# Layer 1 of a two-layer graph network: the sixth gather of a block becomes a table product, ScalarE makes half of the selection matrices, and the bias products change places

## What is computed

```python
h = jnp.maximum(_layernorm(x, axis=-1), 0.0)
x = x + segment_sum(h[src] * edge_weight[:, None], dst)            # layer 0
h = jnp.maximum(_layernorm(x, axis=-1), 0.0)
# layer 1, for each edge e with source row h[src] = (s: 8 scalars, v: 8 vectors of 3)
hid = relu(edge_attr_32 @ W1 + b1)                                 # 32 -> 64
w = (hid @ W2 + b2).reshape(e, 4, 8, 8)                            # 64 -> 256: four 8x8 matrices
m0 = ALPHA * (einsum('ei,eio->eo', s * sh0, w_000) + C110 * einsum('eim,em,eio->eo', v, sh1, w_110))
m1 = ALPHA * (einsum('ei,em,eio->eom', s, sh1, w_011) + einsum('eim,eio->eom', v * sh0, w_101))
x = x + concat(segment_sum(m0, dst), segment_sum(m1, dst)) + self-interaction of h
```

## Time and profile before

| | us |
|---|---|
| median of 3 runs | 6377.49 |
| lowest, highest | 6376.77, 6378.89 |
| the profiled execution, its own time | 6384.63 |
| its span, first to last instruction | 6382.8 |

### The profile page before, as it was taken

One profiled execution on the slowest core, in us unless ns is written; L12 is line 12 of the kernel. 1 busy time (PEld: TensorE's weight loads), 2 busy tenths in 40 slices (PEclk: granted clock), 3 DMA queues, 4 the chain that ended last, 5 costly groups with the idle time before them and its releaser, 6 DMA issues.

```text
span 6382.8 us, 156934 instructions
## 1 busy us (share of the span) xinstructions
PE 6036.7 (95%) x42909; PEld 4954.4 (78%) x42909; DVE 5681.9 (89%) x13211; ACT 2874.3 (45%) x12179; POOL 4754.2 (74%) x5071
## 2 busy tenths in 40 slices
PE   5999999999999999996999999999999999999998
PEld 5888888888888888884777777777777777777775
DVE  7888887777778777776999999999999999999997
ACT  2222222222222222225556556556565565555655
POOL 4777777777777777776777777777777777777776
PEclk9999999999999999997999999999999999999998
DMA  4111111111111111112111111111111111111111
GB/s 109 34 34 34 34 34 34 32 33 34 34 34 34 32 33 34 34 30 45 38 38 38 40 39 38 39 38 38 39 38 38 40 39 39 39 38 38 39 38 34
DMA packets 293179, 243.21 MB, mean 38 GB/s; under 512 B 106611, under 2 KB 289619, under 8 KB 292679
## 3 DMA queue, kind: packets, MB, share of 16 engines
q0 software_dynamic: 158848, 81.65, 9.5%
q1 hardware_dynamic: 133500, 158.02, 9.3%
q10 hardware_dynamic: 802, 3.22, 0.2%
HBM read 237.26 MB, written 5.25 MB: 38 GB/s over the span
## 4 chain that ended last, share of the span: by engine, by line
DVE 26%; PE 25%; POOL 24%; issue 21%; DVEq 3%; DMA 1%; POOLq 1%; ACT 0%; SPq 0%; ACTq 0%
POOL z L464 24%; PE w_ps L705 11%; PE hp_ps L856 6%; DVE prod L1189 5%; DVE p L1174 4%; PE w_ps L786 3%; DVE t L1205 3%; DVE z L1240 3%; DVE prod L1181 3%; DVE reduced_sb L1151 2%; DVE vsh L1167 1%; DVE reduced_sb L1150 1%; DVE prod L1210 1%; DVEq L1002 1%; DVE acc L1009 1%
## 5 line engine op out<-in xcount | busy, mean ns | idle before, releaser
L464 POOL DMA_INDIRECT z<-h_table,idx x4964 | 4710.1, 949 | 1556.6 <-issue 1473.9
L705 PE MATMUL w_ps<-parts,pick 128*128 128x448 f32 x12180 | 2561.6, 369 | 69.5 <-DVE pick L1019 65.6
L705 PEld LDWEIGHTS w_ps<-parts,pick 128*128 128x128 f32 x12180 | 2268.5, 188 | 278.7 <-issue 75.3
L566 ACT ACTIVATE z<-z,squares 128x32 f32<-128x32 f32 x3132 | 726.8, 309 | 2064.6 <-DMA z<-h_table,idx 1951.8
L856 PE MATMUL hp_ps<-parts,pick 128*128 128x448 f32 x6020 | 1341.4, 373 | 32.2 <-DVE squares L1233 29.6
L856 PEld LDWEIGHTS hp_ps<-parts,pick 128*128 128x128 f32 x6020 | 1096.7, 188 | 269.2 <-DVE squares L1233 126.4
L786 PE MATMUL w_ps<-w_sb,squares 64*128 64x256 f32 x6264 | 1088.0, 386 | 0.7 <-ACT squares L617 0.7
L786 PEld LDWEIGHTS w_ps<-w_sb,squares 64*128 64x128 f32 x6264 | 921.9, 194 | 60.2 <-ACT squares L617 1.2
L1019 DVE TENSOR_TENSOR pick<-sc_ps,feat 128x896 fp32r<-128x896 f32 x870 | 911.4, 1081 | 3.6 <-PE w_ps L705 3.6
L1181 DVE TENSOR_TENSOR prod<-w_ps,squares 128x384 f32<-128x384 f32 (+1 forms) x1044 | 781.0, 748 | 0.7 <-ACT squares L623 0.7
L620 ACT ACTIVATE scalars<-z 128x48 f32<-128x48 f32 x522 | 150.9, 289 | 1307.9 <-DMA z<-h_table,idx 1307.8
(11 more groups left out here) (91 smaller groups left out, 4716.4 us busy)
## 6 DMA issues: line engine op xcount, KB each, us to landing
z<-h_table,idx POOLq DMA_INDIRECT x4964, 2.4
squares<-in_ft_sh SPq DMA_DIRECT2D x261, 216.0 KB
feat<-key_table SPq DMA_DIRECT2D x260, 192.0 KB
feat<-key_table SPq DMA_DIRECT2D x260, 128.0 KB
h_table<-big SPq DMA_DIRECT2D x10, 280.0 KB
rel_sb<-in_dst_t SPq DMA_DIRECT2D x1, 1566.0 KB, 10.8
idx_all<-in_src_t SPq DMA_DIRECT2D x1, 1530.0 KB, 9.0
squares<-in_ew_t SPq DMA_DIRECT2D x1, 1530.0 KB, 12.6
```

Source lines behind the costliest of these rows:

```text
L464: pool.indirect_dma_start(z[:, r, u, :], None, rows, bass.IndirectOffsetOnAxis(ap=idx[:, r, u:u + 1], axis=0)).then_inc(z_in[r], 16)
L566: last = nc.scalar.activation(z[:, r, u, :], z[:, r, u, :], ACT.Copy, scale=ew_all[:, bass.ds(n * G + u, 1)])
L705: mm = pe.matmul(fold_ps[:, pick_banks[k], 0:NC * D], pick[:, k, blk, :], parts[:, t, :, blk, :], start=(blk == 0 and t == 0), stop=(blk = ...
```

## The change

Five edits, all in layer 1.

1. Table product in every step: `on_pe` and PE1 are gone. POOL fetches five tiles in the sixth step of a block too; PE, `select` and `sum_groups1` work in all six.
2. Selection matrices by two engines: those of the steps 1, 3 and 5 of a block are made by ACT (`rows_away`: seven activations of 128x128, minus the distance of row number and key, then one of 128x896, relu of one minus that distance), those of steps 0, 2 and 4 by DVE as before. `pick` is used as a ring of three slots in place of five.
3. The comparison `group1_hot` moves from `select` to the head of DVE's step, behind `vsh`.
4. All three biases of a step run on `halves[q]`, in the order third bank, bank 1 - q, then the hidden product, then bank q. The wait for `wts_used` goes ahead of the hidden product, and PE waits for its own bias (`bias_put`) behind the first weight product.
5. SP loads the keys in two lots of three, after waits for two selection matrices each.

```diff
-PE1 = R1 - 1
+RING1 = 3
...
+    def pick_by_act(r):
+        return r % 2 == 1
+    def pick_turn(b, r):
+        return (b - 1) * (R1 // 2) + r // 2 + 1
...
     def arrivals(b, r):
-        return 16 * (G + b * (GT if on_pe(r) else G))
+        return 16 * (G + b * GT)
...
                     if s is None or s >= R1:
-                        sp.wait_ge(pick1_ready, nth(b, 0) + at + count)
-                        sp.nop(nofuse=True)
-                    load_keys1(n - r + R1, at, count)
+                        for t in (at + 1, at + 2):
+                            sp.wait_ge(pick1_by_act if pick_by_act(t) else pick1_by_dve, pick_turn(b, t))
+                            sp.nop(nofuse=True)
...
             def tiles1(r, s):
-                return GT if on_pe(r) and (s is None or s >= R1) else G
+                return GT if s is None or s >= R1 else G
...
+            def rows_away(b, t, s):
+                act.wait_ge(keys1_in[t // BATCH], b * 16)
+                if s is None or s + 4 >= R1 + RING1:
+                    act.wait_ge(picked1, nth(b, t) - RING1 + 1)
+                off = pick[:, t % RING1]
+                for blk in range(GB):
+                    last = nc.scalar.activation(off[:, blk, :], key1[:, t], ACT.Abs, scale=-1.0, bias=rows_sb[:, blk:blk + 1])
+                last.then_inc(rows_off, 1)
+                act.wait_ge(rows_off, pick_turn(b, t))
+                nc.scalar.activation(off, off.bitcast(F32), ACT.Relu, scale=-1.0, bias=one_sb[:]).then_inc(pick1_by_act, 1)
...
                     copy_indices(n + R1, r, idx1_ready)
+                bt, t = before(b, r, R1, -4)
+                if pick_by_act(t) and (s is None or R1 <= s + 4 < S):
+                    rows_away(bt, t, s)
...
                 tile_weights(q, 2, turn, halves[turn], 2, False).then_inc(half_ready, 1)
+                pe.wait_ge(bias_put, n + 1)
...
                     bias(q, 2, halves[q])
+                    if s is None or s >= 2:
+                        pe.wait_ge(wts_used, n - 1)
+                    bias(q, 1 - q, halves[q]).then_inc(bias_put, 1)
...
                         hidden((r + 1) % R1).then_inc(hidpre_ready, 1)
-                    if s is None or s >= 2:
-                        pe.wait_ge(wts_used, n - 1)
                     bias(q, q, halves[q])
-                    bias(q, 1 - q, halves[1 - q])
...
-                if on_pe(t) and (s is None or R1 <= s + 2 < S):
+                if s is None or R1 <= s + 2 < S:
...
-                            mm = pe.matmul(picked_ps, pick[:, t, blk, :], parts[:, p, :, blk, :],
+                            mm = pe.matmul(picked_ps, pick[:, t % RING1, blk, :], parts[:, p, :, blk, :],
...
                         ALU.mult).then_inc(prod_step, 1)
+                mark()
                 step(1)
...
-                nc.vector.tensor_tensor(group1_hot[:], iota_sb[:, 0:NC], group_of[:, bass.ds(b * R1 + r + 2, 1)].to_broadcast([P, NC]),
-                                        ALU.is_equal).then_inc(group1_step, 1)
                 dve.wait_ge(picked1, i + 1)
...
-                    if on_pe((r + 4) % R1) and (s is None or R1 <= s + 4 < S):
+                    if not pick_by_act((r + 4) % R1) and (s is None or R1 <= s + 4 < S):
                         make_pick1(b, r, s)
```

More of the change, by code:

```diff
@@ L250, in gnn_two_layers @@
         table1_in, split1_act, split1_dve = sem("table1_in"), sem("split1_act"), sem("split1_dve")
-        pick1_ready, picked1, group1_step, selected1 = (
-            sem(n) for n in ("pick1_ready", "picked1", "group1_step", "selected1"))
+        pick1_by_dve, pick1_by_act, rows_off, picked1, group1_step, selected1 = (
+            sem(n) for n in ("pick1_by_dve", "pick1_by_act", "rows_off", "picked1", "group1_step", "selected1"))
         idx1_ready, z1_in = (sems(n, R1) for n in ("idx1_ready", "z1_in"))
@@ L282, in groups @@
                         body(g * GU + k, k, False, g)
-        assert JG * D == P and G == 6 and 4 * WN == 1024 and 3 * BATCH > PE1 > BATCH
+        assert JG * D == P and G == 6 and 4 * WN == 1024 and R1 == 2 * BATCH == 2 * RING1 and SLOTS >= RING1
         def stage_columns(op, n, k, js, staged):
@@ L421, in load1 @@
                     sp.dma_start(ft_sh_sb[:, r // 2, :], ft_sh[pair]).then_inc(ft_in[r // 2], 16)
[L423 to L426, removed]
                 if r >= R1 - 2 and (s is None or s - r + R1 < S):
+                    at = 0 if r == R1 - 2 else BATCH
                     if s == R1 - 2:
@@ L640, in prepare @@
                         act.wait_ge(wts_used, m - 1)
-                    if on_pe(v) and (t is None or t >= R1):
+                    if t is None or t >= R1:
                         act.wait_ge(selected1, nth(bv, v) + 1)
@@ L782, in bias @@
             def bias(q, k, rows):
-                pe.matmul(weight_bank(q, k), ones_sb[rows, :], b2_rows[rows, :], start=True, stop=False)
+                return pe.matmul(weight_bank(q, k), ones_sb[rows, :], b2_rows[rows, :], start=True, stop=False)
             def tile_weights(q, k, place, rows, column, stop):
@@ L850, in edge_layer @@
                         pe.wait_ge(split1_dve, 2)
-                    pe.wait_ge(pick1_ready, i + 1)
+                    pe.wait_ge(pick1_by_act if pick_by_act(t) else pick1_by_dve, pick_turn(bt, t))
                     if s is None or s + 2 > R1:
@@ L878, in wide_weights @@
                 pe.nop(nofuse=True)
-                for k in range(3):
-                    bias(0, k, halves[k % 2])
+                bias(0, 0, halves[0])
+                bias(0, 2, halves[0])
+                bias(0, 1, halves[1]).then_inc(bias_put, 1)
                 weights(n + S, 0, 0).then_inc(wts_ready, 1)
@@ L1152, in reduce_sums, with products @@
                                                AX, ALU.add)
-            def products(n, r, q, v, place, select, reduce):
+            def products(n, r, q, v, place, mark, select, reduce):
                 def step(i):
@@ L1251, in place, with mark @@
                         base.append(first_column(n - 3))
-                selects = on_pe((r + 2) % R1) and (s is None or R1 <= s + 2 < S)
+                selects = s is None or R1 <= s + 2 < S
+                def mark():
+                    if selects:
+                        mark_group1(n)
                 def select():
@@ L1275, in layer1 @@
                 if s is None or s < S:
-                    products(n, r, q, r % 3, place, select, reduce)
+                    products(n, r, q, r % 3, place, mark, select, reduce)
                 else:
@@ L1283, in wide_messages1 @@
                 dve.wait_ge(wide_in[1], (n + 1) * 48)
-                products(n + S, 0, 0, 0, lambda: None, lambda: None, lambda: None)
+                products(n + S, 0, 0, 0, lambda: None, lambda: None, lambda: None, lambda: None)
             def wide_reduce(turn):
```

20 lines of the change are left out of this document (11 added, 9 removed).

## The result

The changed kernel takes 6274.35 us (median of 5 runs, 6261.23 to 6323.1) against 6377.48: ratio 0.9847, 95% interval 0.9828 to 0.9866. The forecast was 6272.5 us, with a range of 6266 to 6305.

What follows compares the result with a forecast made beforehand. POOL and DVE were taken to bound layer 1's block together at 38.89 us; after the change POOL's 37.62 plus 0.05 gives 37.67, so 86 blocks gain 105 us: 6377.5 - 105 = 6272.5 us, range 6266 to 6305.

Steps and rivals of the forecast that it cites:

- POOL 37.62 us: Layer 1 loop: POOL's floor for a block of six steps, 30 gathers of 1.254 us, after losing one gather.
- 31 x 1.254 = 38.87 us: Layer 1 before the change: POOL's time for a block's 31 gathers, running without a stop.
- Below 6266 there is nearly nothing: Whole kernel time: claimed that POOL's floor, 6377.5 - 108 = 6269.5 us, leaves almost no chance below 6266.
- near ties jam: Rival, layer 1: PE at 6.34 us or DVE's uneven steps give 38.0 to 38.3 us a block, 6301 to 6327; chance 0.13.
- The late relu: ACT's matrix delays the next step's relu about 1 us every second step; PE, a step of lead, absorbs it.
- DVE 36.90 us: Layer 1: DVE's block after losing two matrices, gaining one selection and moving the comparison; at most 37.5.
- PE 6.26 us: Layer 1: PE's step with the new bias order, down from 6.46 us (6.24 to 6.34); block 37.56 us.
- PE keeps its 6.46 us: Rival: hidden product waits behind the second bias; 38.76 us a block, 11 us gained, 6366; chance 0.12.
- The wait for the bias, 0.02 us: PE's new wait for its own bias in each layer 1 step: cost 0 to 0.10 us, taken as 0.02.
- ACT 3.3 us: ACT's selection matrix every second step: eight activations, 3.3 us (2.6 to 5.4), covered by ACT's present waiting.
- The rival where ACT makes the kernel slower: Layer 1: ACT sets the pace, slower from 5.0 us a matrix, 6475 at 5.4; chance 0.07, including other new waits.
- The added 0.05 us for three near floors: Added to the largest block floor, since POOL, PE and DVE lie near: 37.62 becomes 37.67 us.

Runs made afterwards that it cites:

- e5: Changed kernel with both DVE products of two SBUF operands (last product, `vsh`) replaced by one-operand reduces, leaving out the multiplications by sh: 6257.54 us, ratio 0.9813.
- e1: The changed kernel run once more, no edit, five runs: 6260.03 us, ratio 0.9819.
- e2: Changed kernel with ACT's matrix made between the relu and the rows of the same step: 6298.28 us, ratio 0.9875.
- e6: e2 with the edit of e5 (both two-SBUF-operand products made one-operand reduces): 6257.43 us.
- e8: Changed kernel with all six selection matrices made by DVE, none by ACT: 6463.49 us, ratio 1.0136.
- e4: Changed kernel with the group comparison back in its old place, ahead of the selection: 6314.09 us, ratio 0.9901.
- e3: Changed kernel with the biases in their old order and row halves, without the wait for `bias_put`: 6371.24 us, ratio 0.9991.
- e12: Kernel before the change with only the new order and row halves of the three biases and their wait: 6375.6 us, ratio 0.9998.
- e11: e2 with only `vsh` made by a one-operand reduce, the last product keeping two SBUF operands: 6268.88 us, ratio 0.983.
- e10: e2 with the sum over groups moved between the last product and the next `vsh`, whole computation kept: 6294.11 us, ratio 0.987.

## Why the prediction was right, point by point

- **POOL 37.62 us, mis-sized by 0.09 to 0.15 us.** The step "31 x 1.254 = 38.87 us" took the mean distance of the earlier trace rows as a constant. It held one long gather a block. The mean distance without long gathers is 1.251 us (e5), and 1.249 in e1, so the floor is 37.53 or 37.47 us and the gain up to about 120 us instead of 108. "Below 6266 there is nearly nothing" is therefore wrong: two of the five runs, and all of e1, lie there.
- **POOL's gathers were taken as independent of DVE.** That is the step that failed in the profiled execution: 167 long gathers are 55 us. Its block of 38.15 us lies in the range of the rival "near ties jam", but not by its mechanism: DVE's uneven steps and a PE of 6.34 us weren't needed, POOL itself got longer. The late relu (below) came with it. That long gathers make a block this much longer is shown for e2 against e6, where the two products are the only difference; for the four untraced runs of the changed kernel it is inferred. What puts one execution into the collisions (167) and another beside them (5) isn't known.
- **DVE 36.90 us, right.** Its undisturbed steps are 5.658 us (e1) and 6.646 us (e8), forecast 5.65 and 6.65. e4 (38.12) and e8 (39.87) make DVE the bound and give the sum of the terms within 0.03 us. The busy share is the poorer sign: 98% in the profiled execution as forecast, but 99.6% in e1, whose block leaves DVE 0.56 us. The comparison at the head is free: `vsh` to L1191 is 0.32 us (4554.95 to 4555.27).
- **PE 6.26 us, right.** 6.267 us in the traces with gathers of 0.947 us (median), 6.23 to 6.27 in the others. e3 gives 38.80 us with the old order where the prediction computed 38.76, e12 shows that the new order alone gives nothing: the change needs both. The rival "PE keeps its 6.46 us" is refuted: the hidden product starts 0.005 us (median) after the first bias, in e1 0.004. By the same trace the rule of the Trainium skill, "TensorE: Matmul & The Clock Gate", section "The mechanism", that matmuls keep program order in their starts doesn't hold here across row halves.
- **The wait for the bias, 0.02 us.** Not measured by itself; it is within the 6.267.
- **ACT 3.3 us, right** (3.13). Its seven small activations write the distance of row number and key itself, not minus the distance. The rival where ACT makes the kernel slower is out.
- **The late relu, "PE can take it up", half right.** In e1 the hidden product is delayed by 0.03 us on average in the steps concerned, in the profiled execution by 0.22. The sentence was argued from PE's lead over a whole step; where POOL is late, ACT starts late, and the lead is gone. In e6, with the relu ahead of the matrix, the time is that of e5: no cost of its own is left to it.
- **The added 0.05 us for three near floors** was too much: e1's block is 37.47 us, POOL's floor itself.

The parts and their order are right, but that the median came within 2 us of 6272.5 is luck: two errors of opposite sign lie in it, a floor too high by 0.09 to 0.15 us a block, and no allowance for gathers that DVE stretches. In e1, where nearly none is stretched, the same code comes out 12 us below the forecast and below its range.

## What to carry to other kernels

When an engine that "never stops" is the bound, look at the spread of its instruction and not only at its mean: a few long ones at always the same index are a collision with a fixed place of another engine's step, and they belong to the bound. Such a collision can also hide a bound: in e4 and e8 a gather is held at the same place of every second, or every, step of DVE, so POOL falls back just as far as it would run ahead, and shows no wait although DVE sets its pace. A change that brings two loops close to a common period (10 gathers are 12.51 us, two PE steps 12.53) may lock such a collision in or out; that this is why the same code runs 1% apart is argued, not shown. And before giving an edit its own worth, ask which engine it frees: of the change's parts, undoing the biases costs nearly all of the gain (e3 against e1), undoing ACT's half 1.7 times the gain (e8) and undoing the comparison's place about half (e4), though the biases alone gain nothing (e12). No run puts the gather alone back.

## What the runs showed of the hardware that wasn't expected

- A gather that GpSimd issues is held while VectorE runs an operation with both operands in SBUF: up to 0.22 us by one of 0.22 us alone (e11, 0.944 to 1.161), up to 0.45 us by two in a row (the changed kernel, 0.947 to 1.393), and at most 0.49 us by two and the comparison behind them (e8, 0.944 to 1.434). With reduces of one operand and the same shapes, the longest gather was 1.008 us (e6) instead of 1.384 (e2). The Trainium skill, "SBUF — State Buffer", section "Who interferes with whom", says that a VectorE instruction with two SBUF inputs contends with a GpSimd instruction that reads SBUF; the runs agree, if a gather counts as one. The same section reports that a `tensor_tensor` didn't stall a DMA in a probe, and infers that it takes the shared read interface alone, while the making of descriptors needs the write interface; here the gather that GpSimd issues is held, by up to 0.45 us, and the measurement decides. Which access of the gather is held wasn't tried. Only a part of it can be: in the profiled execution none that starts earlier than 0.27 us ahead of `vsh` is long, though such a gather, too, runs beside both products.
- Spreading the two operations apart halves the hold and doubles the places where it is met (e2 against e10); it took away the extreme values, and little of the sum.
- Two PE products on different row halves can start in another order than the program has, but the semaphore of the one that overtook doesn't seem to be raised ahead of its turn: in the kernel before, `half_ready` is updated 0.12 us behind the modelled end of its product, where most others come 0.014 us behind (those of the window sums 0.10), and 0.03 us behind the end of the bias that the product had overtaken. In the changed kernel, where no bias is overtaken by that product, it is 0.014 us. This was read from traces only.
